# A decoder layer on one core: second up products by column halves, and the expert copies divided anew over three engines

## The chip, the cores and the metric

The kernel runs on one core of a Trainium2 chip. The metric is the device time of one execution in microseconds (us), the median of several runs; lower is better. The engines are TensorE (PE in the profile, its weight loads PEld), VectorE (DVE), ScalarE (ACT), GpSimd (POOL) and SyncE (SP, here only a DMA queue). An engine's name with a q behind it is that engine's own sequencer: register loads, waits, branches.

## The reference

16 sequences of 256 rows and 256 columns pass one decoder layer, all float32. What matters here is its third part, a mixture of 64 experts with two layers. Four rows of 256 make one token of 1024 values, so a sequence has 64 tokens.

```python
def kmoe(x_flat, W_router, A, B, scale, bias, d_in1, d_in2, d_out1, d_out2, top_k):
    logits = x_flat @ W_router.T
    vals, idx = jax.lax.top_k(logits, top_k)
    probs = jax.nn.softmax(vals, axis=-1)
    xs = x_flat.reshape(-1, d_in1, d_in2)
    Ag = A[idx]
    Bg = B[idx]
    Y = jnp.einsum('nkoi,nij,nkpj->nkop', Ag, xs, Bg)
    out = jnp.einsum('nkop,nk->nop', Y, probs).reshape(-1, d_out1 * d_out2)
    return out * scale + bias
...
x = x + _L0_attn_ref(_layernorm(x, axis=-1), ...)    # Fourier mixing, running sum over rows
x = x + _L0_xattn_ref(_layernorm(x, axis=-1), ctx_1024, ctx_1024, ...)    # 16 heads of 64
x = x + _L0_ffn_ref(_layernorm(x, axis=-1), ...)    # kmoe up 32x32 to 64x64, gelu, kmoe down
```

Each token picks two experts (k = 0, 1) in the up layer and two in the down layer. For each, a first product with B (32x64 up, 64x32 down) and a second with A are made, weighted by the softmax of the two logits.

## The kernel before, in words

Everything stays in SBUF but the rows in and out. The loop is staggered: one pass does the attention parts of sequence b and the expert parts of sequence c = b - 1. The list ORDER, written out by hand, sets the order of all steps; each engine walks through the list and does its own share of each step, in that order, so an engine that waits holds back all its later steps. A pass falls into four stretches, named here for the rest of the document:

- the start: `k_proj`, the layer norms, `logits_up`, `route_top_up`, `f_proj`, `route_up`, `product_kv`
- the up stage: steps `("up", g)` for g from 0 to 17, with `("choose", (g + 3, 0))` behind each, and single steps of the attention beside them (`v_proj`, `Q`, `inverse`, `power`, `fpower`, `x1`, `ln2_stats`, `ln2`, `ln2_turn`, `q_proj`)
- `logits_dn`, 32 matmuls of 64 columns over the hidden values `h`
- the heads: steps `("head", i)` for i from 0 to 19, with the down layer between them: `choose` (from i = 2, half of a group at each), `dn_first` at odd i from 5, `dn_second` at even i from 6; then the products with `wo` and `final`

The up layer has 16 groups of 4 tokens. A group's experts are gathered by copies inside SBUF: `choose_up` makes 8 copies (unit = 2 * token + k) of 32 partitions by 128 elements from `experts` into one of 5 buffers `chosen_up`, at a column that comes from a register. The registers are filled by `fetch_offsets`, one load for four groups, in the engine's own sequencer (L246). CHOOSERS divides the units: POOL takes unit 0, DVE 1 to 3, ACT 4 to 7. Then in `up(c, g)`:

- PE makes the first product of group g, two float32 records on 128x128 (L777), into one of three banks FA, FB, S0
- DVE weighs it by the route probabilities into W (`weigh`, L1019)
- PE, two steps later, makes the second product (L788): for each k one matmul of 128 rows by 64 columns with 256 moving columns, summed over k, into partitions 0 to 63 or 64 to 127 of bank G by the group's parity
- DVE scales it and adds the bias into `pre` (L1032, 64 partitions by 256)
- ACT makes the gelu twice into `h`, once plain (L560) and once shifted (L563)

A float32 matmul shows in the trace as two records, so L788 has four in a group. The down layer has 8 groups of 8 tokens; `choose_dn` copies 16 units of 64 partitions by 64 elements, DVE 0 to 7 and ACT 8 to 15, four of each in either half of the step. Its first products (L801) use the two row halves in turn, its second ones (L815) have 32 output columns. `head` on DVE masks the scores (L908), copies every second transposed block of probabilities for PE (L901) and normalises; on PE it transposes (L690), makes scores (L717, L719) and the products with the values (L701 to L704).

GpSimd makes the roots of the layer norms (`deviation`, L388 and L390), half of the Fourier products (`cross`, L404 to L413), `fpower_root`, two bias sums, and its one copy of each up group. `hold(engine, passed, sem, value)` is a wait on a semaphore followed by an increment of `passed`: the engine's sequencer goes no further until the value is there.

Of the kernel before, what the change touches and what calls it, by code (L numbers as in the profile page):

```python
# [23 lines left out]
ACT = mybir.ActivationFunctionType  # L24
# [48 lines left out]
def decoder_layer(nc, t, out):  # L73
    ctx = ExitStack()
    with ctx:
# [25 lines left out]
        experts_up, experts_dn = experts[0:D1, :], experts[F1:P, 0:EXPERTS * 2 * D1]  # L101
# [39 lines left out]
        pre_both = sb("pre", [P, UP_TOK * F1])  # L141
        pre = [pre_both[i * F1:(i + 1) * F1, :] for i in (0, 1)]
# [9 lines left out]
        yT = sb("yT", [P, CT, SEQ])  # L152
        W = [sb(f"W{i}", [P, A_DN // 2]) for i in (0, 1)]
# [7 lines left out]
        route_diag = sb("route_diag", [F1, 2 * TOKENS * TOPK])  # L161
# [57 lines left out]
        FFN_LOADS = 9  # L219
# [33 lines left out]
        def choose_up(copy, held, g, units):  # L253

            to = chosen_up[g % UP_SLOTS]
            for unit in units:
# [4 lines left out]
                src = experts_up[:, bass.ds(held[g % LOADED, unit], 2 * F1)]  # L261
# [66 lines left out]
        def _(sp):  # L328
# [33 lines left out]
            for dst, name in ((experts_up, "experts_up"), (experts_dn, "experts_dn"), (bias_up[:, :], "bias_up"),  # L362
# [13 lines left out]
        def _(pool):  # L376
            pool.memset(vals[:, :, :, KEY:KEY + 1], 1.0).then_inc(vals_ones, 1)
# [7 lines left out]
            def deviation(b, k):  # L385
# [4 lines left out]
                pool.tensor_tensor(rstd[:, k, :], var_eps[:, k, :], inv_root[:, :], ALU.pow).then_inc(ln_rstd[k], 1)  # L390

            def fpower_root(b):
# [4 lines left out]
                pool.tensor_scalar(fnorm[:, :], fnorm[:, :], 1e-9, None, ALU.add).then_inc(fnorm_step, 1)  # L397

            def cross(b, k, left, left_sem, left_n, right):
# [13 lines left out]
                pool.memset(prodA[0:1, 256:512], 0.0).then_inc(lane_fixed, 1)  # L413

            def bias_x1(b):
# [22 lines left out]
            def route_up(c):  # L438
                hold(pool, passed, offsets_ready, at(c, 2, 1))

            steps = {"choose": choose, "route_up": route_up,
# [4 lines left out]
                     "fpower": fpower_root, "ln2_turn": bias_x1, "logits_up": bias_x2}  # L446
# [3 lines left out]
        def _(act):  # L450
# [103 lines left out]
            def up(c, g):  # L554
                g -= UP_SKEW
                if g < 0:
                    return
                act.wait_ge(hidden_in, at(c, 16, g + 1))
                cols = slice(g * UP_TOK * F1, (g + 1) * UP_TOK * F1)
                act.activation(h[0:F1, cols], pre[g % 2], ACT.Gelu).then_inc(h_ready, 1)  # L560
# [558 lines left out]
```

## Time and profile before

| | |
|---|---|
| time, median of 3 runs | 2172.82 us (2169.03 to 2178.83) |
| the profiled execution's own time | 2180.39 us |
| its span, first to last instruction | 2178.5 us |
| mean granted TensorE clock | 0.927 of full speed |
| PE busy | 1947.4 us (89%) |
| DVE busy | 1283.8 us (59%) |
| ACT busy | 1252.4 us (57%) |
| POOL busy | 277.6 us (13%) |

Busy time is the union of an engine's instructions; the records of matmuls run into one another and their ends are modelled. A full pass lasts about 132 us and there are 15 of them with both halves, one half pass ahead and one behind.

### The profile page before, as it was taken

To read this page: it belongs to the slowest core of one execution; us is meant where nothing else is said; L and a number is where in the kernel's file an instruction comes from. 1 tells how busy PE (TensorE), PEld (TensorE's weight loads), DVE (VectorE), ACT (ScalarE), POOL (GpSimd) and SP (SyncE) were. 2 spreads that over 40 slices of the span, in tenths; PEclk is the share of its full clock that TensorE was granted. 3 is DMA by queue.
4 is the path that set the end of the run, shared out by engine and by line. 5 is a ranking of instruction groups with operands and counts; after the bars stand their busy time and mean duration, and the time that the engine had idled before them with its cause. 6 is when DMAs were issued, how large, how long until landed. Compare 5 with 4: busy or idle time off the path is not lost.

```text
span 2178.5 us, 47368 instructions
## 1 busy us (share of the span) xinstructions
PE 1947.4 (89%) x13298; PEld 1458.5 (67%) x13298; DVE 1283.8 (59%) x5457; ACT 1252.4 (57%) x4007; POOL 277.6 (13%) x593
## 2 busy tenths in 40 slices
PE   7998988989898989988989889888989999899975
PEld 5767667675766757667676676767767577675754
DVE  1456555666565666656565556665656656566664
ACT  2475564757556485564755547565474755648553
POOL 3020200203021030200202002020110302102010
PEclk9998999999999898989989899898998989989887
DMA  7000000000000000000000000000000000000000
GB/s 226 1 11 1 7 11 8 11 2 16 2 7 11 7 11 1 7 11 8 11 2 7 11 8 11 2 16 2 7 11 2 16 2 7 11 7 2 1 6 6
DMA packets 18600, 27.65 MB, mean 13 GB/s; under 512 B 2178, under 2 KB 17027, under 8 KB 17923
## 3 DMA queue, kind: packets, MB, share of 16 engines
q1 hardware_dynamic: 18274, 23.84, 3.4%
q8 instruction: 140, 2.29, 0.4%
q14 instruction: 186, 1.52, 0.2%
HBM read 19.65 MB, written 4.19 MB: 11 GB/s over the span
## 4 chain that ended last, share of the span: by engine, by line
PE 63%; DVE 14%; issue 12%; ACT 4%; DVEq 3%; POOL 2%; ACTq 1%; POOLq 0%
PE G L788 7%; PE O L732 5%; PE G L759 5%; PE PT L690 4%; PE G L815 4%; PE S L719 3%; PE S L717 3%; PE S L632 3%; DVE chosen_dn L275 2%; PE S L642 2%; DVE yT L1042 2%; DVE shared L908 2%; PE FA L801 2%; PE PT L672 2%; ACT chosen_up L262 1%
## 5 line engine op out<-in xcount | busy, mean ns | idle before, releaser
L508 ACT ACTIVATE shared<-shared,neg_max 128x128 f32<-128x128 f32 (+1 forms) x512 | 204.9, 447 | 297.8 <-DVE neg_max L908 296.4
L262 ACT COPY chosen_up<-experts 32x128 f32 x1024 | 251.6, 291 | 44.9 <-issue 38.5
L788 PE MATMUL G<-chosen_up,W 128*64 128x256 f32 x1024 | 260.5, 394 | 8.0 <-DVE pre L1032 8.0
L908 DVE CUSTOM_DVE_ANT_0 shared<-S,neg_bias 128x128 f32<-128x128 f32 (+1 forms) x512 | 162.4, 355 | 127.7 <-PE S L719 122.1
L690 PE MATMUL PT<-ident,shared 128*128 128x128 f32 x768 | 161.0, 326 | 77.9 <-DVE shared L901 65.1
L275 ACT COPY chosen_dn<-experts 64x64 f32 x1024 | 197.7, 240 | 52.9 <-issue 36.5
L275 DVE COPY chosen_dn<-experts 64x64 f32 x1024 | 152.4, 189 | 67.6 <-issue 57.5
L262 DVE COPY chosen_up<-experts 32x128 f32 x768 | 171.9, 255 | 32.3 <-issue 27.1
L388 POOL TENSOR_SCALAR var_eps<-moments 128x2 f32<-128x2 f32 x48 | 10.4, 217 | 1355.7 <-DVE moments L845 1345.5
L1032 DVE SCALAR_TENSOR_TENSOR pre<-G,scale_up,bias_up 64x256 f32<-64x256 f32 x256 | 123.2, 481 | 87.5 <-PE G L788 79.8
L815 PE MATMUL G<-chosen_dn,W 128*32 128x64 f32 x2048 | 157.5, 237 | 18.5 <-DVE W L1019 18.5
L1042 DVE COPY yT<-G 32x64 f32<-32x64 f32 x512 | 111.6, 218 | 100.5 <-PE G L815 86.9
L690 PEld LDWEIGHTS PT<-ident,shared 128*128 128x128 f32 x768 | 95.6, 162 | 110.7 <-issue 86.4
L788 PEld LDWEIGHTS G<-chosen_up,W 128*64 128x64 f32 x1024 | 113.0, 137 | 79.5 <-DVE W L1019 9.8
L815 PEld LDWEIGHTS G<-chosen_dn,W 128*32 128x32 f32 x2048 | 135.0, 121 | 33.9 <-issue 16.1
L467 ACT ACTIVATE kT<-S,bk 128x256 f32<-128x256 f32 x64 | 26.9, 470 | 193.8 <-PE S L609 193.8
L560 ACT ACTIVATE h<-pre 64x256 f32<-64x256 f32 x256 | 106.1, 415 | 34.9 <-DVE pre L1032 28.7
L759 PEld LDWEIGHTS G<-r_dn,h 128*64 128x64 f32 x1024 | 115.0, 204 | 6.8 <-issue 5.0
L732 PE MATMUL O<-wo,qT 128*128 128x256 f32 x512 | 118.7, 385 | 0.0
L759 PE MATMUL G<-r_dn,h 128*64 128x64 f32 x1024 | 117.2, 276 | 1.4 <-ACT h L563 1.4
L948 DVE MAX8 top_val<-G 64x8 f32<-64x64 f32 x32 | 7.2, 225 | 175.4 <-PE G L759 139.1
L262 POOL COPY chosen_up<-experts 32x128 f32 x256 | 78.3, 315 | 245.3 <-PE G L788 228.3
(164 smaller groups left out, 3819.4 us busy)
## 6 DMA issues: line engine op xcount, KB each, us to landing
x<-in_x SPq DMA_DIRECT2D x16, 256.0 KB, 2.7
ctxT<-in_ctxT SPq DMA_DIRECT2D x16, 256.0 KB, 2.9
out<-xn SPq DMA_DIRECT2D x16, 256.0 KB, 3.1
neg_bias<-in_neg_bias SPq DMA_DIRECT2D x1, 2048.0 KB, 13.3
wk<-in_xWk SPq DMA_DIRECT2D x1, 1024.0 KB
wo<-in_xWo SPq DMA_DIRECT2D x1, 1024.0 KB
wv<-in_xWv SPq DMA_DIRECT2D x1, 1024.0 KB, 7.7
wq<-in_xWq SPq DMA_DIRECT2D x1, 1024.0 KB, 9.7
```

What stands on the lines that cost most here:

```text
L262: last = copy(dst, src.rearrange("p (m c) -> p m c", m=2))
L275: last = copy(dst, src.rearrange("p (m c) -> p m c", m=2))
L508: act.activation(probs[i % 3][:, lo:hi], probs[i % 3][:, lo:hi], ACT.Exp, bias=neg_max[:, i % 3, rt:rt + 1], scale=-1.0).then_inc(probs_re ...
L560: act.activation(h[0:F1, cols], pre[g % 2], ACT.Gelu).then_inc(h_ready, 1)
L690: mm = pe.transpose(PT[:, j * P:(j + 1) * P], probs[e % 3][:, j * P:(j + 1) * P], ident[:, :])
L732: mm = pe.matmul(O[:, rt * 256:(rt + 1) * 256], qT[:, m, rt * P:(rt + 1) * P], wo[:, m, :], start=(m == 0), stop=(m == PAIRS - 1))
L759: mm = pe.matmul(G[0:F1, 0:EXPERTS], cols[:, 0, q, :], r_dn[:, q, :], start=(q == 0), stop=(q == F1 // 2 - 1))
L788: mm = pe.matmul(G[g % 2 * F1:(g % 2 + 1) * F1, 0:n], up_W(g)[:, k * F1:(k + 1) * F1], chosen_up[g % UP_SLOTS][:, k * n:(k + 1) * n], star ...
L815: mm = pe.matmul(G[g % 2 * F1:g % 2 * F1 + D1, u * 2 * D1:(u + 1) * 2 * D1], W[g % 2][:, n * D1:(n + 1) * D1], chosen_dn[g % DN_SLOTS][:, ...
L908: dve.tensor_tensor_reduce(probs[i % 3][:, lo:hi], S[i % 2][:, lo:hi], neg_bias[:, i, (1 - rt) * P:2 * P], 1.0, TOP, ALU.add, ALU.min, neg ...
L1032: dve.scalar_tensor_tensor(pre[g % 2].rearrange("p (n o) -> p n o", o=F1), G[side, 0:n].rearrange("p (n o) -> p n o", o=F1), scale_up[side ...
L1042: dve.tensor_copy(yT[il * D1:(il + 1) * D1, :, g * rows:(g + 1) * rows], y[:, il]).then_inc(y_kept, 1)
```

## The change

1. The second up products are made for two neighbouring groups at once, at every odd step: four matmuls, of which the first and third write partitions 0 to 63 of G and the other two partitions 64 to 127. The `pre` of both groups is then one DVE instruction on 128 partitions, and ACT makes four gelus in a row. `pre` now lies in `yT`. PE gets a wait for W of three groups ago ahead of a first product.
2. The copies are divided anew. Up: POOL units 0 to 3 (tokens 0 and 1), DVE 4 and 5, ACT 6 and 7. Down: by DN_TOKEN, POOL takes the four odd tokens (8 units, partitions 64 to 127), DVE tokens 0 and 2, ACT tokens 4 and 6 (4 units each). The up experts lie twice in `experts`, on partitions 0 to 31 and 32 to 63, and a token's parity picks the copy that is read. There are 6 buffers `chosen_up`.
3. POOL also takes part in the down `choose` (all 8 units in the first half of the step) and has a hold at the end of `deviation`, `fpower_root`, `cross`, the bias sums and each up `choose`, so that it waits for its own last instruction before the next step.
4. `xn3T` is stored by ACT with the four rows of a token apart, so that the weights of `logits_up` are read from neighbouring elements; `own_parts` reads it accordingly. `route_diag` and a block of ones lie in the unused columns of `experts`, and the down offsets are sorted by the new shares.

```diff
-UP_SLOTS, DN_SLOTS = 5, 3
+UP_SLOTS, DN_SLOTS = 6, 3
 UP_SKEW = 2
+UP_PAIRS = UP_GROUPS // 2
...
-CHOOSERS = {"pool": {"up": range(0, 1), "dn": range(0, 0)},
-            "dve": {"up": range(1, 4), "dn": range(0, 8)},
-            "act": {"up": range(4, 8), "dn": range(8, 16)}}
+CHOOSERS = {"pool": {"up": range(0, 4), "dn": range(8, 16)},
+            "dve": {"up": range(4, 6), "dn": range(0, 4)},
+            "act": {"up": range(6, 8), "dn": range(4, 8)}}
+DN_TOKEN = (0, 2, 4, 6, 1, 3, 5, 7)
...
-                src = experts_up[:, bass.ds(held[g % LOADED, unit], 2 * F1)]
+                src = experts_up[n % 2][:, bass.ds(held[g % LOADED, unit], 2 * F1)]
...
             def choose(c, n_part):
 
-                n = n_part[0]
+                n, part = n_part
+                if part == 0:
+                    fetch_offsets(held, mybir.EngineType.Pool, n, "pool")
                 if n < UP_GROUPS:
-                    fetch_offsets(held, mybir.EngineType.Pool, n, "pool")
                     if n >= UP_SLOTS:
                         hold(pool, passed, second_done, at(c, GROUPS, n - UP_SLOTS + 1))
                     choose_up(pool.tensor_copy, held, n, CHOOSERS["pool"]["up"]).then_inc(chosen_pool, 1)
+                    hold(pool, passed, chosen_pool, at(c, GROUPS, n + 1))
+                elif part == 0:
+                    g = n - UP_GROUPS
+                    if g >= DN_SLOTS:
+                        hold(pool, passed, second_done, at(c, GROUPS, n - DN_SLOTS + 1))
+                    choose_dn(pool.tensor_copy, held, g, CHOOSERS["pool"]["dn"]).then_inc(chosen_pool, 1)
+                    if g == DN_GROUPS - 1:
+                        hold(pool, passed, chosen_pool, at(c, GROUPS, n + 1))
...
-                act.copy(xn3T[:, :, :], FA[:, :].rearrange("p (c s) -> p c s", c=CT)).then_inc(xn3T_ready, 1)
+                act.copy(xn3T[:, :, :].rearrange("p c (r n) -> p c n r", r=UP_TOK),
+                         FA[:, :].rearrange("p (c n r) -> p c n r", c=CT, r=UP_TOK)).then_inc(xn3T_ready, 1)
...
-                g -= UP_SKEW
-                if g < 0:
+                pair, odd = divmod(g - UP_SKEW, 2)
+                if pair < 0 or not odd:
                     return
...
-                        rows = xn3T[:, ct, :].rearrange("p (n r) -> p r n", r=UP_TOK)[:, r, :]
-                        mm = pe.matmul(G[0:F1, 0:EXPERTS], rows, r_up[:, n, :], start=(n == 0), stop=(n == 2 * UP_TOK - 1))
+                        mm = pe.matmul(G[0:F1, 0:EXPERTS], xn3T[:, ct, r * TOKENS:(r + 1) * TOKENS], r_up[:, n, :], start=(n == 0), stop=(n == 2 * UP_TOK - 1))
...
-                    pe.wait_ge(chosen_pool, at(c, UP_GROUPS, g + 1))
+                    pe.wait_ge(chosen_pool, at(c, GROUPS, g + 1))
+                    if g >= 3:
+                        pe.wait_ge(W_ready, at(c, GROUPS, g - 2))
...
-                g -= UP_SKEW
-                if g >= 0:
-                    pe.wait_ge(W_ready, at(c, GROUPS, g + 1))
-                    if g >= 2:
-                        pe.wait_ge(hidden_in, at(c, 16, g - 1))
+                pair, odd = divmod(g - UP_SKEW, 2)
+                if pair >= 0 and odd:
+                    pe.wait_ge(W_ready, at(c, GROUPS, 2 * pair + 2))
+                    if pair >= 1:
+                        pe.wait_ge(hidden_in, at(c, UP_PAIRS, pair))
                     else:
                         pe.wait_ge(pm_ready, at(c, 6, 4))
                     n = UP_TOK * F1
                     for k in range(TOPK):
-                        mm = pe.matmul(G[g % 2 * F1:(g % 2 + 1) * F1, 0:n], up_W(g)[:, k * F1:(k + 1) * F1],
-                                       chosen_up[g % UP_SLOTS][:, k * n:(k + 1) * n], start=(k == 0), stop=(k == TOPK - 1))
-                    mm.then_inc(second_done, 1)
+                        for j in (0, 1):
+                            of = 2 * pair + j
+                            mm = pe.matmul(G[j * F1:(j + 1) * F1, 0:n], up_W(of)[:, k * F1:(k + 1) * F1],
+                                           chosen_up[of % UP_SLOTS][:, k * n:(k + 1) * n], start=(k == 0), stop=(k == TOPK - 1))
+                            if k == TOPK - 1:
+                                mm.then_inc(second_done, 1)
...
                 pe.wait_ge(chosen_act, at(c, GROUPS, UP_GROUPS + g + 1))
+                pe.wait_ge(chosen_pool, at(c, GROUPS, UP_GROUPS + g + 1))
...
-                    dve.scalar_tensor_tensor(pre[g % 2].rearrange("p (n o) -> p n o", o=F1),
-                                             G[side, 0:n].rearrange("p (n o) -> p n o", o=F1),
-                                             scale_up[side, 0:1], spread(bias_up[side, :], 1, UP_TOK),
+                    dve.scalar_tensor_tensor(pre[pair % 2].rearrange("p (n o) -> p n o", o=F1),
+                                             G[:, 0:n].rearrange("p (n o) -> p n o", o=F1),
+                                             scale_up[:, 0:1], spread(bias_up[:, :], 1, UP_TOK),
                                              ALU.mult, ALU.add).then_inc(hidden_in, 1)
```

## Rows read from the trace of the kernel before

**Rows 1.** Windows over three passes' heads: length, PE busy, clock, DMA share, GB/s.

```profile
428.52:490.48 61.96, 55.93 (x531) 0.94 0.01 2
1088.01:1154.08 66.07, 60.19 (x531) 0.87 0.01 2
954.31:1021.66 67.35, 61.65 (x531) 0.85 0.01 2
```

**Rows 2.** Windows of 2 us in the heads of one pass, same columns.

```profile
1096.00:1098.00 2.00, 0.00 (x1) 0.97 0.00 0
1098.00:1100.00 2.00, 1.53 (x9) 0.50 0.00 0
```

**Rows 3.** Timeline, same heads: start, us, instruction, count, idle time before and its releaser.

```profile
1097.13 0.64 DVE L275 COPY chosen_dn<-experts 64x64 f32 x4 [1.79 <-issue]
...
1098.47 0.90 PE L690 MATMUL PT<-ident,shared 128*128 128x128 f32 x3 [2.47 <-DVE shared L901]
...
1124.48 0.54 PE L690 MATMUL PT<-ident,shared 128*128 128x128 f32 x3 [1.88 <-DVE shared L901]
```

**Rows 4.** Line 246, the offset loads: ns min/median/max, first and last start, of each sequencer.

```profile
L246 ACTq TENSOR_LOAD <-offsets x96: 1009/1022/1969, 115.0 to 2150.7; - x96
L246 DVEq TENSOR_LOAD <-offsets x96: 845/858/2104, 115.1 to 2154.9; - x96
L246 POOLq TENSOR_LOAD <-offsets x64: 315/321/522, 117.0 to 2116.6; - x64
```

**Rows 5.** Chain that ended last, 428 to 492 us: shares by line.

```profile
by line: issue 16.6%; PE O L732 11.4%; DVE chosen_dn L275 7.5%; DVE yT L1042 5.9%; DVE shared L908 5.7%; PE PT L690 4.3%; PE S L719 4.2%; PE S L717 3.9%; PE G L815 3.2%; PE FA L672 3.0%; PE FB L672 3.0%; DVEq L246 2.7%; PE FA L801 2.6%; PE 
```

**Rows 6.** Window over one up stage: us, busy PE, PEld, DVE, ACT, POOL, clock, DMA.

```profile
1045.50:1080.70 35.20, 32.18 (x142) 18.66 (x140) 24.82 (x88) 31.32 (x99) 9.91 (x24) 1.00 0.05 16
```

**Rows 7.** Chain in the same up stage: start, us, what.

```profile
1055.46 0.42 PE S L777 x2
1055.88 1.01 PE G L788 x4
```

**Rows 8.** Timeline of PE in the heads: products on one or on two halves.

```profile
1088.26 0.60 PE L719 MATMUL S<-kT,qT 64*128 64x256 f32 x4
...
1111.22 0.68 PE L801 MATMUL FB<-chosen_dn,h 64*64 64x64 f32 x16
...
1114.23 1.08 PE L815 MATMUL G<-chosen_dn,W 128*32 128x64 f32 x16
```

**Rows 9.** Timeline of POOL, start and up stage.

```profile
1044.16 0.99 POOL L262 COPY chosen_up<-experts 32x128 f32 x2 [0.26 <-issue]
1045.86 1.24 POOL L404 TENSOR_TENSOR shared<-shared 128x256 f32<-128x256 f32 x1 [0.70 <-DVE shared L867]
...
1049.00 0.80 POOL L262 COPY chosen_up<-experts 32x128 f32 x3
...
1062.14 0.70 POOL L395 TENSOR_TENSOR fnorm<-fpower,root 128x2 f32<-128x2 f32 x1 [0.98 <-DVE fpower L882]
...
1063.89 0.28 POOL L262 COPY chosen_up<-experts 32x128 f32 x1 [0.30 <-issue]
...
1069.05 0.29 POOL L262 COPY chosen_up<-experts 32x128 f32 x1 [1.56 <-PE G L788]
```

**Rows 10.** Timeline of DVE beside POOL's products, then line 262's range on DVE.

```profile
1046.43 1.57 DVE L262 COPY chosen_up<-experts 32x128 f32 x3
...
L262 DVE COPY chosen_up<-experts x768: 203/216/749, 116.3 to 2124.3; 32x128 f32 x192
```

**Rows 11.** Groups of the whole trace, gelus: busy us, mean ns, idle before.

```profile
L560 ACT ACTIVATE h<-pre 64x256 f32<-64x256 f32 x256 | 106.1, 415 | 34.9 <-DVE pre L1032 28.7
...
L563 ACT ACTIVATE h<-pre 64x192 f32<-64x192 f32 x256 | 92.3, 360 | 6.2
```

**Rows 12.** Timeline of PE: the two logits.

```profile
1033.90 2.13 PE L752 MATMUL G<-r_up,xn3T 128*64 128x64 f32 x16
...
1080.68 5.52 PEld L759 LDWEIGHTS G<-r_dn,h 128*64 128x64 f32 x49 [0.33 <-issue]
```

More of the change, by code:

```diff
@@ L152, in decoder_layer @@
         yT = sb("yT", [P, CT, SEQ])
+        pre = [yT[:, i, :] for i in (0, 1)]
         W = [sb(f"W{i}", [P, A_DN // 2]) for i in (0, 1)]
@@ L218, in decoder_layer @@
         ATTN_LOADS = 4
-        FFN_LOADS = 9
+        FFN_LOADS = 10
         block = ctx.enter_context(nc.Block())
@@ L390, in deviation @@
                 pool.tensor_tensor(rstd[:, k, :], var_eps[:, k, :], inv_root[:, :], ALU.pow).then_inc(ln_rstd[k], 1)
+                hold(pool, passed, ln_rstd[k], at(b, 2, 2))
             def fpower_root(b):
@@ L397, in fpower_root @@
                 pool.tensor_scalar(fnorm[:, :], fnorm[:, :], 1e-9, None, ALU.add).then_inc(fnorm_step, 1)
+                hold(pool, passed, fnorm_step, at(b, 2, 2))
             def cross(b, k, left, left_sem, left_n, right):
@@ L413, in cross @@
                 pool.memset(prodA[0:1, 256:512], 0.0).then_inc(lane_fixed, 1)
+                hold(pool, passed, lane_fixed, at(b, 6, 3 * k + 3))
             def bias_x1(b):
@@ L419, in bias_x1 @@
                 pool.tensor_tensor(x1[:, :, :], x1[:, :, :], spread(out_bias[:, :], 1, RT), ALU.add).then_inc(x1_biased, 1)
+                hold(pool, passed, x1_biased, at(b, 1, 1))
             def bias_x2(c):
@@ L436, in choose, with route @@
                     choose_up(pool.tensor_copy, held, n, CHOOSERS["pool"]["up"]).then_inc(chosen_pool, 1)
-            def route_up(c):
-                hold(pool, passed, offsets_ready, at(c, 2, 1))
-            steps = {"choose": choose, "route_up": route_up,
+                    hold(pool, passed, chosen_pool, at(c, GROUPS, n + 1))
[6 more added lines that the diff above has]
+                        hold(pool, passed, chosen_pool, at(c, GROUPS, n + 1))
+            def route(c, layer):
+                hold(pool, passed, offsets_ready, at(c, 2, layer + 1))
+            steps = {"choose": choose, "route_up": lambda c: route(c, 0),
                      "ln1": lambda b: deviation(b, 0), "ln3": lambda c: deviation(c, 2),
@@ L554, in up @@
             def up(c, g):
[L555 to L556 removed]
+                pair, odd = divmod(g - UP_SKEW, 2)
+                if pair < 0 or not odd:
                     return
[L558 to L563 removed]
+                act.wait_ge(hidden_in, at(c, UP_PAIRS, pair + 1))
+                for j in (0, 1):
+                    cols = slice((2 * pair + j) * UP_TOK * F1, (2 * pair + j + 1) * UP_TOK * F1)
+                    hidden = pre[pair % 2][j * F1:(j + 1) * F1, :]
+                    act.activation(h[0:F1, cols], hidden, ACT.Gelu).then_inc(h_ready, 1)
+                    above = h[F1:P, cols].rearrange("p (u c) -> p u c", c=2 * F1)[:, :, 0:2 * F1 - F1 // 2]
+                    shifted = hidden.rearrange("p (u c) -> p u c", c=2 * F1)[:, :, F1 // 2:2 * F1]
+                    act.activation(above, shifted, ACT.Gelu).then_inc(h_ready, 1)
             steps = {"k_proj": k_proj, "ln1_turn": lambda b: keep_xnT(b, 1), "f_proj": f_proj, "v_proj": v_proj,
@@ L972, in route_keep @@
                 of = G[0:1, 256:384].rearrange("p (g u) -> p g u", g=groups)
+                by_half = G[0:1, 256:384].rearrange("p (g t half k) -> p half g t k", g=groups, half=2, k=TOPK)
                 for name in CHOOSERS:
@@ L976, in route_keep @@
                         to = offsets[:, start:start + groups * len(units)].rearrange("p (g u) -> p g u", g=groups)
-                        last = dve.tensor_copy(to, of[:, :, units.start:units.stop])
+                        if layer == 0:
+                            last = dve.tensor_copy(to, of[:, :, units.start:units.stop])
+                        else:
+                            half, first = divmod(units.start // TOPK, DN_TOK // 2)
+                            some = by_half[:, half, :, first:first + len(units) // TOPK, :]
+                            last = dve.tensor_copy(to.rearrange("p g (t k) -> p g t k", k=TOPK), some)
                 last.then_inc(offsets_ready, 1)
```

40 lines of the change are left out of this document (20 added, 20 removed).

## The prediction

> **What bounds the kernel now.** I read the page first. It puts TensorE far ahead of the others, but a full pass is made of stretches with different limits, and two of them are touched.
>
> The heads come first. Windows over the heads of three passes [rows 1] show the same work in 61.96, 66.07 and 67.35 us; what differs is the granted clock: 0.94, 0.87, 0.85. Between the levels 2.4 and 1.2 GHz a mean clock of 0.94 is 12% of the stretch at the low one, 7.4 us; 0.85 is 30%, 20.2 us. So 12.8 us more at the low level cost 5.4 us, 0.42 us each, and the middle row agrees (17.2 us low, 66.1 forecast). With no low clock the heads would take 61.96 - 3.1 = 58.9 us. The windows of 2 us [rows 2] show what went before: TensorE did nothing for 2 us, then the clock stood at 0.50. The timeline [rows 3] names the cause: DVE's down copies start after 1.79 us of issue, L901 behind them is late, and TensorE waits 2.47 us for it; eight heads later the same again, 1.88 us. The 1.79 us are the offset load of 32 values in DVE's sequencer [rows 4]. Where no load falls, the chain of waits through the heads [rows 5] runs over DVE as much as over PE: its down copies are 7.5% of it.
>
> The up stage is different: PE is busy 32.18 of 35.20 us at clock 1.00, ACT 31.32, DVE 24.82 and POOL only 9.91 [rows 6]. A group costs PE 0.42 us for the first product and 1.01 us for the second [rows 7], so 16 groups are 22.9 of the 32.2 us; the rest is the attention's. In its second half ACT, with two gelus (0.415 and 0.360 us [rows 11]) and four copies a group, is as long as PE.
>
> **The change, part by part.** Everything is counted against the profiled execution: 2180.4 us, of which 2178.5 are span; the median of the runs is 7.6 us lower.
>
> Column halves. In the heads, where neighbouring products use different halves of the array, 16 records of L801 take 0.68 us, while 16 of L815, all on one part of the columns, take 1.08 [rows 8]; in L719 four records with 256 columns on two row halves take 0.60 us, against 1.01 for four of L788. No row shows halves of columns alone. If they overlap like the row halves, a pair costs 0.95 to 1.1 us instead of 2.02; if not, 2.02 as now. I take 1.0. Per pass PE loses 8 x 1.0 = 8 us of work in the up stage, and DVE makes 8 `pre` on 128 partitions for 16 on 64. This is a gain only as far as no other engine sets the pace.
>
> Who sets it then. Per group ACT has two copies fewer, about 0.8 + 0.5 = 1.3 us; DVE one fewer and half a `pre`. POOL has four copies for one. From its rows [rows 9]: three copies in a row take 0.80 us, 0.26 apart, so four take 1.05; after a hold and a wait the next copy starts some 0.30 us later. A group is 1.35 us. The load of 16 values, by 60 ns a value (ACT 16 to 32 values, 1.009 to 1.969 us [rows 4]) on top of POOL's 0.32 for 4, is 1.04 us, and with the new hold nothing covers it. None of this is queued behind PE: the sixth buffer leaves POOL free to run ahead. So POOL's own queue sets the stage, and I follow it in the times of the pass shown. Its copies began at 1044.16. The load adds 0.7 and the hold 0.15; the earlier Fourier products (below) take back 0.5: 1044.5. Group 0 beside DVE's running sums, where two copies took 0.99 [rows 9], takes 1.5, group 1 1.35: 1047.4. Then `product_q` is ahead of group 2 in the queue, 1045.86 to 1049.00 before, 3.14 us: 1050.7 with its hold. 14 groups at 1.35 are 18.9, three loads 3.1, `fpower_root` 1.2 (1062.14 to the copy before the one at 1063.89): 1073.9.
>
> What contention adds is bounded from below by nothing. From above: beside POOL's Fourier products DVE's three copies took 1.57 us, 0.52 each [rows 10], against a median of 0.216, so the two engines do hold each other up. DVE now has two copies of 0.22 a group; if POOL meets each of them half way, 0.15 to 0.2 a group, 2.1 in all. The last copy ends at 1076.0 instead of 1069.34 [rows 9]. The Trainium skill (SBUF — State Buffer, "Who interferes with whom") states that a VectorE copy of this kind and a GpSimd operation lock one port pair for the whole instruction, the loser fully blocked; the 0.52 us agree, and by a full block of every DVE copy by POOL the sum would only gain 0.2 us a group more.
>
> Behind the last copy. Before, 11.3 us passed from it to `logits_dn` (1069.34 to 1080.68 [rows 9, 12]). PE then still had five second products, 5.05 us; now it has two pairs, 2.0. But `ln2` stands on POOL behind the last `choose`, and DVE waits there for the root, with all its later weighing: root and small operation 1.17, as in `fpower_root`, and DVE's norm 0.8, 2.0 us in which PE has no work. 11.3 - 3.05 + 2.0 = 10.3. So `logits_dn` starts at 1086.3, 5.6 later than now; with some low clock after PE's many short waits I take 6.0 per pass, 96 us for 16. Four gelus in a row, 1.55 us, lie beside the last `q_proj`.
>
> Start. L752's 16 records take 2.13 us [rows 12], against 1.08 for L815's [rows 8] with weights side by side in memory: 1.0 us less on PE. ACT's copies into `own` stand between this and the Fourier products, so I count half, already used above. ACT's spread write of `xn3T` and the other read pattern in `own_parts` I take at nothing: same element counts; were they a tenth longer, 0.4 us of ACT there, under what is left over.
>
> Heads. DVE's load falls from 32 to 16 values: 1.259 us for 20 values [rows 4], 63 ns each, so 1.0 us less; and two of four copies at 0.16 go [rows 3], 0.3. Both idle times of PE shrink by 1.3 us, to 1.2 and 0.6. The up stage has 3.0 us idle at clock 1.00 throughout [rows 6], so I expect the clock to hold: 66.1 - 7.2 - 2.6 = 56.3 us. POOL now has 8 copies a group (under 0.28 each, 2.1 us and two loads of 2.0) in some 5.3 us of heads, covered by its idle time; `dn_first` of a group comes three heads after its `choose`. It will meet DVE's copies, 0.8 us. Sum -9.0 a pass, bounds -2.6 (the clock still falls) and -11 (DVE's 16 other copies a pass, 2.6 us on its part of the chain, are won as well); 15 passes, -135 us.
>
> Sum: 2180.4 + 96 - 135 = 2141.4, less 7.6: 2134 us.
>
> **The rivals.**
> - GpSimd's copies are cheaper than their pitch of 0.26 us. For: units 0 and 1 use partitions 0 to 31, units 2 and 3 partitions 32 to 63, and all its rows are on 0 to 31. If the pairs overlap, four take 0.7 us, 14 x 0.35 = 4.9 us a pass less, up stage +1.1: 2180.4 + 18 - 135 - 7.6 = 2055. The Trainium skill (GPSIMD Engine Reference, "Instruction dispatch") states that each of its cores serves 16 partitions and goes to the next instruction when its own share is done, which would give this result; no run here shows it yet.
> - The other side: GpSimd is slower still. For: the pair at 1044.16 took 0.50 us a copy [rows 9]. If copies average 0.33, the stage loses another 14 x 0.28 = 4 us, +10, and PE, waiting at every group, falls to the low clock before the heads, which then win only 6: 2180.4 + 160 - 90 - 7.6 = 2243. It decides from +8.4 us in the up stage on, where a group costs 0.17 us more than I count.
> - The heads keep the low clock, because 1.2 us idle still suffices or POOL's copies lengthen it. Then they win 2.6 us: 2134 + 15 x 6.4 = 2230; one of the two falls avoided, 2182. Against: PE's idle time halves in one and falls to a third in the other.
> - The change doesn't do what it says, the column halves run one after the other: two pairs behind the last copy cost 2.1 us more, 2134 + 34 = 2168; the rest hides behind POOL.
>
> **How the numbers follow.** Forecast 0.40, cheap GpSimd 0.18, slow GpSimd 0.17, low clock kept 0.18, no overlap 0.07. A change within 0.5% (2162 to 2184) is about what this kernel's measurement can't tell from none. The forecast's own range, 2095 to 2175, is mostly faster (0.36) with 0.03 in the band and 0.01 slower; cheap GpSimd is 0.18 faster; no overlap 0.02, 0.04 and 0.01; low clock 0.02, 0.05 and 0.11; slow GpSimd 0.17 slower. Together 0.58, 0.12, 0.30. The range 2045 to 2235 takes in the forecast, both halves of the low clock and parts of the two GpSimd cases.
>
> **What would show it.** Right: L788 in pairs of some 1.0 us for eight records; PE in the up stage waiting for POOL's `chosen_up`, POOL busy nearly throughout it; the stage 5 to 7 us longer; the offset loads near 1.1 us on DVE and 1.0 and 2.0 on POOL; idle times of 1.2 and 0.6 us ahead of L690 and heads near 57 us at clock 1.00; L752's weight loads near 0.11 us. Wrong: POOL's copies far from 0.26 us apart in the up stage, or a clock under 0.9 in the heads.

## The result, and the profile after

The changed kernel takes 2233.3 us (median of 4 runs, 2223.26 to 2236.03), the kernel before 2175.75 us beside it (4 runs): a ratio of 1.0245, 95% interval 1.0214 to 1.0276. It is slower; 2134 us was forecast. The profiled execution took 2233.06 us, its span is 2231.3 us.

The page first, with parts 1, 2 (PE and its clock) and 4:

```profile
PE 1882.9 (84%) x13298; PEld 1419.6 (64%) x13298; DVE 1130.3 (51%) x4577; ACT 1029.6 (46%) x2983; POOL 662.5 (30%) x2387
PE   7979788897898979889798897988979788797965
PEclk9988979889798988989889798897989889888977
...
PE 47%; issue 18%; POOL 13%; DVE 9%; POOLq 5%; ACT 4%; DVEq 1%
POOL chosen_up L264 8%; PE G L780 5%; PE O L754 5%; PE G L842 5%; PE PT L712 4%; PE S L741 3%; PE S L739 3%; POOLq L248 3%; PE G L813 2%; PE O L631 2%; DVE yT L1074 2%; PE PT L694 2%; DVE shared L935 2%; PE FA L828 2%; POOL rstd L395 2%
```

VectorE and ScalarE lost 150 and 220 us of work, GpSimd gained 385, and GpSimd's up copies now lead the chain. To see where the time went, the windows over one pass, cut at the first `logits_up`, the first up product, `logits_dn`, the first head, `final` and the next `logits_up` (us, busy PE, PEld, DVE, ACT, POOL, clock, DMA share, GB/s):

```profile
1059.72:1072.44 12.72, 10.85 (x52) 7.25 (x51) 6.91 (x28) 9.04 (x25) 4.53 (x10) 1.00 0.00 1
1072.44:1112.39 39.95, 30.26 (x141) 18.30 (x141) 16.81 (x62) 23.08 (x67) 21.36 (x70) 0.83 0.04 14
1112.39:1119.72 7.33, 7.33 (x66) 7.26 (x66) 0.00 (x0) 2.09 (x3) 0.00 (x0) 1.00 0.01 2
1119.72:1182.72 63.00, 58.65 (x531) 47.74 (x532) 39.00 (x175) 25.81 (x85) 11.84 (x64) 0.89 0.01 2
1182.72:1197.04 14.32, 10.37 (x46) 8.20 (x44) 8.02 (x22) 4.15 (x8) 3.19 (x5) 0.88 0.07 22
```

Cut the same way, from the starts of these lines in each trace, the means over the 15 full passes are below ("end" is from `final` to the next `logits_up`, a mean of 14). The rows below the first two are experiments of the next section. One of e7's five executions (2092.83 us), the one with the trace, ran disturbed at a lower clock; it doesn't count in e7's ratio, and e7 has no row here. "Low" is the part of the up stage and of the heads, in us, that TensorE spent at 1.2 GHz.

| kernel | start | up stage | low | heads | low | end | time, us |
|---|---|---|---|---|---|---|---|
| before | 11.60 | 35.25 | 0.2 | 66.14 | 17.3 | 12.43 | 2175.75 |
| after | 12.82 | 40.03 | 14.6 | 62.11 | 12.3 | 14.07 | 2233.3 |
| e1 down copies held | 12.77 | 40.49 | 16.9 | 54.77 | 0.0 | 13.12 | 2118.57 |
| e9 down copies drained | 12.78 | 40.46 | 16.0 | 55.71 | 1.8 | 13.46 | 2133.14 |
| e8 = e1, no norm hold | 12.81 | 40.33 | 16.2 | 54.77 | 0.0 | 12.54 | 2108.5 |
| e5 = e1, single products | 12.77 | 38.86 | 1.8 | 55.04 | 0.9 | 12.84 | 2089.4 |
| e6 = e5, old up shares | 11.60 | 35.21 | 0.5 | 55.03 | 0.9 | 14.20 | 2042.14 |
| e10 = e6, no norm hold | 11.60 | 35.64 | 1.8 | 55.03 | 0.9 | 13.56 | 2038.02 |
| e11 = e10, old layout | 11.60 | 35.59 | 0.5 | 56.34 | 3.9 | 13.87 | 2061.03 |
| e12 = e10, pairs | 11.61 | 36.41 | 15.5 | 54.73 | 0.0 | 12.63 | 2029.43 |
| e2 = after, single products | 12.84 | 39.04 | 2.7 | 62.06 | 12.1 | 14.17 | 2228.31 |
| e3 = after, old division | 11.60 | 36.56 | 17.5 | 65.69 | 17.8 | 13.33 | 2210.26 |
| e4 = after, old layout | 13.43 | 41.21 | 20.0 | 61.38 | 10.7 | 14.38 | 2253.75 |

After against before, a full pass: start +1.2, up stage +4.8, heads -4.0, end +1.6; 15 x 2.0 + 14 x 1.6 = 53 us, the difference of the two spans (52.8).

**The heads.** The timeline of the same pass, POOL, DVE and PE, answers to [rows 3]:

```profile
1125.87 4.36 POOL L278 COPY chosen_dn<-experts 64x64 f32 x24 [21.32 <-issue]
...
1127.84 2.44 DVE L278 COPY chosen_dn<-experts 64x64 f32 x2 [0.78 <-issue]
1130.20 0.54 DVE L928 COPY shared<-PT 128x384 f32<-128x384 f32 x1
...
1130.88 0.54 PE L712 MATMUL PT<-ident,shared 128*128 128x128 f32 x3 [3.10 <-DVE shared L928]
1131.48 0.80 PE L739 MATMUL S<-kT,qT 64*128 64x128 f32 x4
...
1157.08 0.54 PE L712 MATMUL PT<-ident,shared 128*128 128x128 f32 x3 [0.55 <-DVE shared L928]
```

VectorE's issue time fell from 1.79 to 0.78 us, as forecast. But GpSimd finds its first three buffers free and makes all their 24 copies in one run; VectorE's two copies come 2 us into it and take 2.44 us. L928 (L901 before) is late, TensorE waits 3.10 us for it, more than the 2.47 of before, and behind it L739 takes 0.80 us, where a head earlier it took 0.49: the clock is at 1.2 GHz. Eight heads later the wait is 0.55 us, and the clock stays at 1.00 from there to the end of the heads. The instructions of the line that copies, ns min/median/max:

```profile
L278 POOL COPY chosen_dn<-experts x1024: 229/248/306, 173.7 to 2219.1; 64x64 f32 x171
...
L278 DVE COPY chosen_dn<-experts x512: 177/189/2434, 175.7 to 2221.8; 64x64 f32 x171
```

Fifteen of VectorE's 512 copies last 2107 to 2434 ns, one in each full pass; a sixteenth, in the last half pass, 709.

**The up stage.** Timeline of POOL (it answers to [rows 9]) and PE, in order of time:

```profile
1078.09 0.46 PE L800 MATMUL S<-chosen_up,own 128*128 128x128 f32 x2 [1.53 <-POOL chosen_up L264]
...
1080.60 1.08 POOL L264 COPY chosen_up<-experts 32x128 f32 x4 [1.33 <-issue]
1081.92 1.12 POOL L264 COPY chosen_up<-experts 32x128 f32 x4 [0.24 <-POOL chosen_up L264]
1083.38 1.08 POOL L264 COPY chosen_up<-experts 32x128 f32 x4 [0.34 <-POOL chosen_up L264]
...
1087.49 1.08 PE L813 MATMUL G<-chosen_up,W 128*64 128x256 f32 x8
...
1094.62 0.46 PE L800 MATMUL S<-chosen_up,own 128*128 128x128 f32 x2 [2.29 <-DVE W L1052]
...
1099.25 1.98 PE L813 MATMUL G<-chosen_up,W 128*64 128x256 f32 x8
1100.06 1.08 POOL L264 COPY chosen_up<-experts 32x128 f32 x4 [0.34 <-POOL chosen_up L264]
```

A GpSimd group is 1.08 + 0.34 = 1.42 us, and a load puts about 1.3 us ahead of it. In this pass TensorE waits four times for GpSimd's copies, 4.6 us in all, and once, 2.29 us, for W. L813's eight records take 1.08 us, where four of L788 took 1.01 [rows 7]: the column halves overlap almost fully. At the low clock they take 1.98.

**The end.** Timeline of POOL, ACT and PE:

```profile
1189.37 0.71 POOL L395 TENSOR_TENSOR rstd<-var_eps,inv_root 128x2 f32<-128x2 f32 x1
1190.46 0.22 POOL L393 TENSOR_SCALAR var_eps<-moments 128x2 f32<-128x2 f32 x1 [0.37 <-POOL rstd L395]
1191.68 1.05 ACT L536 COPY xn3T<-FA 128x512 f32<-128x512 f32 x1 [1.15 <-PE FA L763]
1193.34 1.11 PE L644 MATMUL TR<-ident,xn 128*128 128x128 f32 x4 [1.70 <-DVE xn L878]
1194.25 2.86 PE L631 MATMUL O<-ctxT,wk 128*128 128x256 f32 x8
1197.04 1.15 PE L773 MATMUL G<-r_up,xn3T 128*64 128x64 f32 x16
```

The same places of the kernel before (the ACT row is of the pass ahead of this one):

```profile
1030.33 0.59 ACT L517 COPY xn3T<-FA 128x512 f32<-128x512 f32 x1 [0.73 <-PE FA L741]
...
1163.82 0.66 PE L622 MATMUL TR<-ident,xn 128*128 128x128 f32 x4 [1.29 <-DVE xn L851]
1164.31 1.89 PE L609 MATMUL O<-ctxT,wk 128*128 128x256 f32 x8
```

The second norm now waits for GpSimd to finish the first, TensorE waits 1.70 us where it waited 1.29, and then it too runs slower: four records take 1.11 us and took 0.66, the next eight take 2.86 and took 1.89. The spread write of `xn3T` takes 1.05 us, the plain one took 0.59. What the new layout gives is the last row of the upper block, 1.15 us for 2.13 [rows 12]. In the mean of the 14 stretches TensorE is at the low level for 3.1 us, for 0.5 before; in the two that hold 1.00 the end takes 12.8 us, 0.6 more than those of before that hold it (12.2).

### The profile page after: what moved, and what is told of

The parts are those of the page before. It is cut to its first block, busy times and chain, and to the rows that moved or that the text cites. A ratio compares the mean times of both kernels' runs of the same rounds, so it can differ in the third digit from the quotient of the medians.

```text
span 2231.3 us, 47686 instructions
## 1 busy us (share of the span) xinstructions
PE 1882.9 (84%) x13298; PEld 1419.6 (64%) x13298; DVE 1130.3 (51%) x4577; ACT 1029.6 (46%) x2983; POOL 662.5 (30%) x2387
## 3 DMA queue, kind: packets, MB, share of 16 engines
q8 instruction: 140, 2.29, 0.4%
## 4 chain that ended last, share of the span: by engine, by line
PE 47%; issue 18%; POOL 13%; DVE 9%; POOLq 5%; ACT 4%; DVEq 1%
POOL chosen_up L264 8%; PE G L780 5%; PE O L754 5%; PE G L842 5%; PE PT L712 4%; PE S L741 3%; PE S L739 3%; POOLq L248 3%; PE G L813 2%; PE O L631 2%; DVE yT L1074 2%; PE PT L694 2%; DVE shared L935 2%; PE FA L828 2%; POOL rstd L395 2%
## 5 line engine op out<-in xcount | busy, mean ns | idle before, releaser
L278 POOL COPY chosen_dn<-experts 64x64 f32 x1024 | 189.5, 253 | 777.1 <-PE G L842 437.0
L264 POOL COPY chosen_up<-experts 32x128 f32 x1024 | 280.7, 298 | 172.5 <-issue 92.8
L712 PE MATMUL PT<-ident,shared 128*128 128x128 f32 x768 | 153.2, 313 | 62.3 <-DVE shared L928 54.7
L582 ACT ACTIVATE h<-yT 64x256 f32<-64x256 f32 x256 | 106.4, 415 | 214.8 <-DVE yT L1064 210.1
L813 PE MATMUL G<-chosen_up,W 128*64 128x256 f32 x1024 | 181.6, 488 | 0.7 <-DVE yT L1064 0.7
L712 PEld LDWEIGHTS PT<-ident,shared 128*128 128x128 f32 x768 | 91.0, 155 | 91.8 <-issue 62.9
L842 PEld LDWEIGHTS G<-chosen_dn,W 128*32 128x32 f32 x2048 | 126.0, 115 | 25.9 <-DVE W L1052 10.2
L264 ACT COPY chosen_up<-experts 32x128 f32 x512 | 118.5, 292 | 35.7 <-DVE offsets L1006 31.1
L393 POOL TENSOR_SCALAR var_eps<-moments 128x2 f32<-128x2 f32 x48 | 10.4, 217 | 392.1 <-DVE moments L872 372.3
L278 DVE COPY chosen_dn<-experts 64x64 f32 x512 | 109.7, 255 | 31.8 <-issue 25.3
L1064 DVE SCALAR_TENSOR_TENSOR yT<-G,scale_up,bias_up 128x256 f32<-128x256 f32 x128 | 61.7, 482 | 124.1 <-PE G L813 122.6
L264 DVE COPY chosen_up<-experts 32x128 f32 x512 | 105.1, 249 | 23.1 <-issue 15.7
L278 ACT COPY chosen_dn<-experts 64x64 f32 x512 | 98.2, 240 | 34.1 <-PE G L842 20.3
L800 PE MATMUL FA<-chosen_up,own 128*128 128x128 f32 x192 | 55.1, 378 | 65.9 <-POOL chosen_up L264 37.7
```

What stands on the lines that cost most here:

```text
L264: last = copy(dst, src.rearrange("p (m c) -> p m c", m=2))
L278: last = copy(dst, src.rearrange("p (m c) -> p m c", m=2))
L582: act.activation(h[0:F1, cols], hidden, ACT.Gelu).then_inc(h_ready, 1)
L712: mm = pe.transpose(PT[:, j * P:(j + 1) * P], probs[e % 3][:, j * P:(j + 1) * P], ident[:, :])
L813: mm = pe.matmul(G[j * F1:(j + 1) * F1, 0:n], up_W(of)[:, k * F1:(k + 1) * F1], chosen_up[of % UP_SLOTS][:, k * n:(k + 1) * n], start=(k = ...
L842: mm = pe.matmul(G[g % 2 * F1:g % 2 * F1 + D1, u * 2 * D1:(u + 1) * 2 * D1], W[g % 2][:, n * D1:(n + 1) * D1], chosen_dn[g % DN_SLOTS][:, ...
```

## The experiments

**1. The down copies held back (e1).** GpSimd begins a down group only when VectorE has made its copies of it, so its first 24 copies no longer come in one run.

```diff
                     if g >= DN_SLOTS:
                         hold(pool, passed, second_done, at(c, GROUPS, n - DN_SLOTS + 1))
+                    hold(pool, passed, chosen_dve, at(c, GROUPS, n + 1))
```

> Edit: GpSimd starts its down copies of a group only when VectorE has made its own of that group. Theory (GpSimd's 24 copies in a row keep VectorE's down copies waiting 2.44 us, TensorE then idles 3.10 us and its clock falls): the pair of VectorE copies takes 0.3 us, TensorE's wait ahead of L712 shrinks to 1.0 to 1.3 us, the clock holds in the heads, heads about 57.5 instead of 62.3 us a pass: 2233 - 15 x 4.8 = 2161 us. Rival (an idle time of 1.2 us lets the clock fall as well): only the 1.9 us of idle time go, 2205 us. Rival (VectorE is late for its own offset load): no change, 2233 us.

Measured 2118.57 us, ratio 0.9718 (0.9666 to 0.977). The line's row on VectorE, and the clock in the heads, with e5's window (the same hold) for a look at the columns:

```profile
L278 DVE COPY chosen_dn<-experts x512: 179/190/261, 178.1 to 2108.1; 64x64 f32 x171
```

```profile
1060.00:1114.60 54.60, 52.49 (x530) 42.81 (x531) 36.82 (x175) 25.69 (x85) 11.95 (x64) 1.00 0.01 2
```

No copy is over 261 ns, the clock stays at 1.00, TensorE's wait ahead of the products of L712 is 0.98 us, and the heads take 54.8 us in every pass. One wait, added, is worth 115 us, where 72 were expected: the heads are 2.7 us shorter than the 57.5 put for them. It also delays GpSimd's copies, so it doesn't yet say whether their meeting VectorE's is the trouble or the length of the run.

**2. Drained after each down group (e9).** GpSimd starts as early as in the changed kernel, but waits for its own last copy after every group.

```diff
-                    if g == DN_GROUPS - 1:
-                        hold(pool, passed, chosen_pool, at(c, GROUPS, n + 1))
+                    hold(pool, passed, chosen_pool, at(c, GROUPS, n + 1))
```

> Edit: the changed kernel with a hold behind each of GpSimd's down groups of 8 copies, not only behind the last, so that its first three groups run as 1.5 us, a pause of 0.3, 1.5 us and so on instead of 4.36 us without a pause. Theory (VectorE's copy can't begin while GpSimd's copies follow one another without a gap, and gets in at the first gap): VectorE's longest down copy falls from 2.4 us to at most 1.5, TensorE's wait of 3.1 us by 0.8 or more; as the clock may still fall, 2190 to 2225 us. Rival (it waits for one GpSimd copy at a time, and something else made it late): no copy changes, 2233 us.

Measured 2133.14 us, 0.9763 (0.9737 to 0.9789), far under what was expected; only in three passes does the clock still fall in the heads, for 7 to 14 us. Timeline of POOL, DVE and PE, the copies' timeline first:

```profile
1093.09 1.48 POOL L278 COPY chosen_dn<-experts 64x64 f32 x8 [21.26 <-issue]
1094.82 1.50 POOL L278 COPY chosen_dn<-experts 64x64 f32 x8 [0.24 <-POOL chosen_dn L278]
1095.06 0.40 DVE L278 COPY chosen_dn<-experts 64x64 f32 x2 [0.78 <-issue]
1096.06 0.54 PE L711 MATMUL PT<-ident,shared 128*128 128x128 f32 x3 [1.06 <-DVE shared L927]
```

And the line's own row on VectorE:

```profile
L278 DVE COPY chosen_dn<-experts x512: 177/189/259, 179.3 to 2125.2; 64x64 f32 x171
```

The copies still meet: VectorE's two start 0.24 us into a GpSimd run and take 0.40 us together. So meeting is harmless; what costs is the long run. In this trace 72 of VectorE's copies start inside a run of 8, all but one at most 0.93 us after its beginning (the one at 1.47, as the run ends), and take 0.19 to 0.26 us. In the changed kernel those in runs of 8 do the same (the longest 0.30 us), and those that start 1.97 us into the run of 24 are held until its last copy. Where between 0.97 and 1.97 us the blocking sets in was not tried. The 24 copies follow each other every 0.177 us, but single ones grow from 0.235 us at the start of a run to 0.26 at its eighth and 0.30 at its twenty-fourth: they overlap more and more. That no gap is left for VectorE is likely, and only argued. The Trainium skill (SBUF — State Buffer, "Who interferes with whom") lets the engine that comes second wait for the whole instruction of the other; by that rule the wait would end after one copy, 0.3 us. The changed kernel's 2.28 us are a wait for all that is left of a run, and the 0.22 and 0.26 us of the two copies shown here are hardly a wait at all.

**3. Single second products (e2 from the changed kernel, e5 from e1).** Second products, `pre` and gelus are made group by group again, as before; the division of the copies stays.

```diff
-                pair, odd = divmod(g - UP_SKEW, 2)
-                if pair >= 0 and odd:
+                g -= UP_SKEW
+                if g >= 0:
...
-                        for j in (0, 1):
-                            of = 2 * pair + j
-                            mm = pe.matmul(G[j * F1:(j + 1) * F1, 0:n], up_W(of)[:, k * F1:(k + 1) * F1],
+                        mm = pe.matmul(G[g % 2 * F1:(g % 2 + 1) * F1, 0:n], up_W(g)[:, k * F1:(k + 1) * F1],
```

> Edit: the new division of the copies with the second up products made group by group as before. Theory (GpSimd sets the pace of the up stage, so the pairs win next to nothing there): the up stage grows by 2 to 3 us for the products behind the last copy, 2265 to 2285 us. Rival (the pairs' saved TensorE work counts in full, 8 us a pass): 2233 + 128 = 2360 us.

> Edit: GpSimd's down copies behind VectorE's, as in the first experiment, and the second up products group by group as before; the division of the changed kernel. Theory (the pairs win nothing: the TensorE time that they save in the up stage comes back as low clock): up stage 39.0 us against 40.5 with pairs, heads 54.8 in both, 2118 - 16 x 1.2 = 2100 us. Rival (the pairs are worth their 8 us of TensorE work where the clock is held): 2118 + 100 = 2220 us.

Measured e2 2228.31 us, 1.0236 (1.0178 to 1.0295), against the changed kernel's 1.0245: no difference clear of noise; e5 2089.4 us, 0.957 (0.9531 to 0.9609), 29 us under e1. Under GpSimd's pace the pairs cost time: the stage is 38.9 us without them and 40.5 with, low for 1.8 and 16.9 us. The loss expected of e2 didn't come. Window of e5's up stage, and its last copies and `logits_dn`:

```profile
1013.60:1052.60 39.00, 33.59 (x140) 19.58 (x140) 20.97 (x70) 23.40 (x66) 21.35 (x70) 0.96 0.04 14
```

```profile
1041.21 1.08 POOL L264 COPY chosen_up<-experts 32x128 f32 x4 [0.34 <-PE G L810]
...
1052.66 1.54 PE L779 MATMUL G<-r_dn,h 128*64 128x64 f32 x12
```

From the end of GpSimd's last copy to `logits_dn` it is 1052.66 - 1042.29 = 10.4 us without pairs and, in the changed kernel, 1112.39 - 1101.14 = 11.25 with them. In the mean of the 15 full passes it is 10.2 in e2 and e5, 11.3 in the changed kernel, 11.5 in e1 and 11.4 in the kernel before.

**4. The old up shares (e6), and two, three, three (e7).** From e5, GpSimd makes one up copy a group again, VectorE three, ScalarE four, and the hold after GpSimd's up copies goes; e7 gives GpSimd 2 and the others 3 each.

```diff
-CHOOSERS = {"pool": {"up": range(0, 4), "dn": range(8, 16)},
-            "dve": {"up": range(4, 6), "dn": range(0, 4)},
-            "act": {"up": range(6, 8), "dn": range(4, 8)}}
+CHOOSERS = {"pool": {"up": range(0, 1), "dn": range(8, 16)},
+            "dve": {"up": range(1, 4), "dn": range(0, 4)},
+            "act": {"up": range(4, 8), "dn": range(4, 8)}}
```

> Edit: e5 with the up copies divided as before the change (GpSimd 1, VectorE 3, ScalarE 4) and no hold behind each up choose; only the down copies are divided anew. Theory (GpSimd's four up copies set the pace of the up stage): up stage 35.2 us as before, clock 1.00, heads 54.8: 2100 - 16 x 4 - 10 = 2030 us. Rival (the longer start and the late layer norms, not the up copies, are what was lost): 2090 us.

> Edit: e6 with GpSimd 2, VectorE 3 and ScalarE 3 up copies. Theory (ScalarE was as long as TensorE in the second half of the old up stage; GpSimd at two copies a group, 0.85 us, has room): up stage 33.5 to 34.5 us, 10 to 25 us under e6. Rival (TensorE's 32.2 us of work and its short waits already fill the stage): the same as e6 within 5 us. Rival (more GpSimd copies lengthen VectorE's): 10 us over e6.

Measured e6 2042.14 us, 0.9379 (0.9313 to 0.9445): 47 us under e5, start -1.2 and up stage -3.7, end +1.4 a pass. The longer end goes with the clock: 3.4 us at the low level for 0.2. e7 2042.89 to 2056.65 us, 0.9384 (0.9335 to 0.9432): no difference from e6. Two, three, three gains nothing over one, three, four; four, two, two costs 47 us, together with the hold behind its copies, which no run takes out alone.

**5. The pairs with the old division (e3).** The changed kernel, with the copies, up and down, divided as before; the new layout stays.

```diff
+CHOOSERS = {"pool": {"up": range(0, 1), "dn": range(0, 0)},
+            "dve": {"up": range(1, 4), "dn": range(0, 8)},
+            "act": {"up": range(4, 8), "dn": range(8, 16)}}
```

> Edit: the pairs with the old division of the copies (GpSimd one up copy, ScalarE four; down copies on VectorE and ScalarE), all else as changed. Theory (eight records of a pair take 1.08 us instead of 2.02, then ScalarE with 31 us of work limits the up stage): up stage 35.2 to about 33 us, heads as before with their two falls of the clock, 66.2 us: 2180 - 2 x 16 + 10 for the slower start = 2150 to 2165 us. Rival (TensorE's work is the limit throughout): up stage 27 us, 2060 us. Rival (longer pairs add waits): 2180 or more.

Measured 2210.26 us, 1.0134 (1.008 to 1.0187), 45 us over the range expected; the rival with 2180 or more is the one that fits. Windows of its up stage and heads:

```profile
525.60:562.40 36.80, 33.04 (x141) 19.74 (x139) 20.61 (x79) 31.64 (x98) 10.05 (x24) 0.72 0.05 15
569.70:635.20 65.50, 60.37 (x531) 48.70 (x531) 39.87 (x206) 31.38 (x117) 0.00 (x0) 0.87 0.01 2
```

ScalarE is busy for 31.6 us, as before (31.32 [rows 6]), so little was to be gained beside it. The work that the pairs save on TensorE becomes short waits, the clock falls to a mean of 0.72 for 1.00, and what is left keeps TensorE busy for 33.04 us, for 32.18. The heads are those of before: the down division alone changes them.

**6. The old layout of `xn3T` (e4 from the changed kernel, e11 from e10).**

```diff
-                act.copy(xn3T[:, :, :].rearrange("p c (r n) -> p c n r", r=UP_TOK),
-                         FA[:, :].rearrange("p (c n r) -> p c n r", c=CT, r=UP_TOK)).then_inc(xn3T_ready, 1)
+                act.copy(xn3T[:, :, :], FA[:, :].rearrange("p (c s) -> p c s", c=CT)).then_inc(xn3T_ready, 1)
...
+                        rows = xn3T[:, ct, :].rearrange("p (n r) -> p r n", r=UP_TOK)[:, r, :]
```

> Edit: only the layout of xn3T as before; all else as changed. Theory: ScalarE's write of xn3T takes 0.59 instead of 1.05 us, the 16 records of logits_up 2.13 instead of 1.15 us; the first lies ahead of TensorE's second turn, the second ahead of the Fourier products, each partly covered: within 8 us of 2233. If the spread write is what makes the start longer: 2233 - 16 x 1 = 2217 us. If the faster logits carry the stage: 2233 + 16 = 2249 us.

> Edit: e10 with the old layout of xn3T as well. Theory (the same edit made the changed kernel 20 us slower: logits_up is a microsecond longer on TensorE while ScalarE's 0.46 us are partly covered): 2032 + 8 to 16 = 2044 us. Rival (with the up stage no longer waiting for GpSimd's start, ScalarE's spread write is what counts): 2025 us.

Measured e4 2253.75 us, 1.0315 (1.0252 to 1.0379); e11 2061.03 us, 0.945 (0.942 to 0.9479), against e10's 2038.02. The new layout is worth 23 us there, clear of noise and more than the 8 to 16 expected. From e4 to the changed kernel it is 20 us by the times and 15 by the ratios, whose intervals just overlap. ScalarE's slower write doesn't show: with the plain one the end is no shorter (14.4 us in e4 for 14.1, 13.9 in e11 for 13.6). In e4 the start is 0.6 and the up stage 1.2 us a pass longer; in e11 neither is, and its heads fall to the low clock in four passes for 13.7 us where e10's do in one. Why, no row shows.

**7. Without the hold at the end of `deviation` (e8 from e1, e10 from e6).**

```diff
-                hold(pool, passed, ln_rstd[k], at(b, 2, 2))
```

> Edit: the first experiment without the hold at the end of deviation. Theory (the hold puts the second root of the layer norms 0.4 us later, at three places of a pass, two of them at the start on the way to TensorE's turns): start 0.4 to 0.8 us a pass shorter, 2118 - 10 = 2108 us. Rival (the start is longer for ScalarE's spread write of xn3T alone): 2118 us.

> Edit: e6 (single second products, old up shares, down copies of GpSimd behind VectorE's) without the hold at the end of deviation. Theory (that hold costs about 0.6 us a pass, as it did in e8): 2042 - 10 = 2032 us. Rival (in e6 the stretch ahead of logits_up is longer for its low clock, and the hold hides): 2042 us.

Measured e8 2108.5 us, 0.966 (0.9622 to 0.9698); e10 2038.02 us, 0.936 (0.9339 to 0.938). The end is 0.6 us a pass shorter in both; that is 10 us in e8, whose four executions all lie below those of e1, and 4 in e10, less than its interval.

**8. The pairs in the best version (e12).** e10 with the second products in pairs, as in the changed kernel.

> The best version so far (2038 us: GpSimd's down copies held behind VectorE's, up shares 1, 3, 4, second up products group by group, no hold at the end of deviation) with one part of the change put back: the second up products in pairs. It tells what the pairs alone do where nothing else differs and the heads are undisturbed. Theory: the pairs overlap fully and take 8 us of TensorE's work out of the up stage, but the engine then has short waits between the pairs, falls to the low clock for 10 to 20 us of the stage, and the stage lasts 36.8 us for 35.1, as in the run with pairs and the old division; heads stay at 54.6. So 15 x 1.7 = 26 us more: 2055 to 2070. Rival: in the earlier run the low clock came from the disturbed pass, not from the pairs; then ScalarE's 31 us set the stage, it takes 32 to 34 us at clock 1.00, and the time is 2000 to 2025.

Measured 2029.43 us, 0.9317 (0.9294 to 0.934). The loss expected didn't come: it is 9 us under e10, and the intervals just touch. Windows of the up stage and the stretch behind the heads of a pass of e12, then of e10:

```profile
610.40:646.00 35.60, 31.31 (x142) 18.67 (x140) 20.69 (x79) 31.59 (x98) 9.51 (x24) 0.76 0.05 16
...
708.10:720.10 12.00, 8.88 (x45) 7.00 (x43) 7.95 (x22) 4.14 (x8) 3.19 (x5) 1.00 0.09 26
```

```profile
491.80:526.90 35.10, 32.05 (x141) 18.71 (x139) 24.34 (x87) 30.83 (x97) 9.96 (x24) 1.00 0.05 16
...
588.80:602.90 14.10, 10.77 (x46) 8.11 (x44) 8.01 (x22) 4.14 (x8) 3.19 (x5) 0.88 0.07 22
```

The up stage is longer, by 0.8 us in the mean, with 15.5 us at the low level, as the theory had it. It overlooked the rest of the pass: the end takes 12.6 us for 13.6, and in the pass shown it holds clock 1.00, where e10's has 0.88 (at the low level for 0.8 us in the mean, for 2.4). So e12 has more low clock than e10, but most of it lies where TensorE waits for ScalarE's copies anyway:

```profile
624.83 0.80 PE L799 MATMUL S<-chosen_up,own 128*128 128x128 f32 x2 [0.90 <-ACT chosen_up L264]
```

Why the end is spared is open. e12 is the fastest version measured, by little: the changed kernel's layout, pairs and down division, the old up shares, one hold added and two taken out.

## Why the prediction was wrong

The wrong step is in "Heads": "It will meet DVE's copies, 0.8 us", and with it "so I expect the clock to hold". The term was -9.0 us a pass and came out at -4.0: 15 x 5.0 = 75 of the 92 us between the sum (2141.4) and the profiled 2233.1. I priced GpSimd's copies by their number and their pitch and let them meet VectorE's one by one; I didn't ask when they would be issued. Three free buffers make it 24 in a row, and one copy of 0.19 us was held for 2.3. The idle time put at 1.2 us was 3.10; the second, put at 0.6, was 0.55. Experiments 1 and 2 show the cause: both break up or shift the run, keep every copy, and bring the heads to 54.8 and 55.7 us, below the 57.1 of the forecast. The rival "heads keep the low clock" had the right place and named GpSimd's copies as a way to it; its 2230 us was near, partly by luck, since it left the next term out.

The second miss is the end, +1.6 us a pass, 23 us, which isn't in the sum at all. The hold at the end of `deviation` is 0.6 us of it by experiment 7: item 3 of the change puts it on the path of both norms. The rest goes with the clock: 2.6 us more at the low level, 1.1 us by the prediction's own 0.42 each, an estimate. Taking ACT's spread write of `xn3T` "at nothing" was right for the time: it is 0.46 us longer, not the tenth allowed for, but the end is no shorter without it (experiment 6).

What was right: GpSimd's queue sets the up stage. Start and up stage together were put at +6.0 and are +1.2 + 4.8. A group was put at 1.35 and takes 1.42; the slow-GpSimd rival needed 0.17 more, not 0.07. The offset loads, put at 1.1 us on DVE and 1.0 and 2.0 on POOL (ns min/median/max):

```profile
L248 DVEq TENSOR_LOAD <-offsets x96: 593/602/1101, 114.8 to 2209.1; - x96
L248 POOLq TENSOR_LOAD <-offsets x96: 1048/1060/2033, 117.2 to 2206.5; - x96
```

The rival by which four GpSimd copies overlap to 0.7 us falls: they take 1.08, both halves of the partitions or not. The down copies, all on partitions 64 to 127, have a pitch of 0.177 us. The rival by which the column halves run one after the other falls too.

Near in size for a wrong reason: "Behind the last copy" lets the pairs save 3.05 us and adds 2.0 for `ln2`, 10.3 us for 11.3. In the mean it is 11.3 us, for 11.4 before, and 10.2 in e2 and e5 without pairs (experiment 3): here the pairs save nothing, and cost 1.0 to 1.3 us. That single second products fit into the waits of TensorE, and that the pairs leave it at the low clock, is the likely reason, not a shown one. The sum came out near because up to the last copy the pass is 6.1 us longer, for the 6.7 of the forecast, and because 0.4 us had been added for a low clock. In the whole study the pairs were worth between -29 us (e5 to e1) and +9 (e10 to e12, where the intervals touch). The gain of the change was the down division, which takes 11.4 us out of the heads once the run is broken up, and the layout.

## What to carry to other kernels

Ask of work that is moved to an idle engine not only how long it takes but when it will be issued: free buffers turn it into one burst, and a burst on GpSimd can hold a short VectorE copy until its end; a wait that costs nothing there was worth 5% here. TensorE time saved in a stretch that another engine sets was no gain in that stretch here, and came back as a lower clock; what it does to the stretches behind must be measured. When a change adds waits "for order", price each on the path it stands in.

## What the runs showed of the hardware

- A VectorE copy of 64x64 float32, 0.19 us alone, took 0.19 to 0.31 us when it started less than 1 us into a run of 8 GpSimd copies, and 2.1 to 2.4 us when it started 1.97 us into a run of 24: until about that run's last copy.
- Float32 products in the two column halves overlapped almost fully: eight records of 256 columns in 1.08 us, four in 1.01.
- GpSimd's copies from a column given by a register: four of 32x128 in 1.08 us, eight of 64x64 in 1.50, and 0.24 to 0.34 us more until the first copy after a hold on its own last one.
- ScalarE's copy of 128x512 from PSUM took 1.05 us with a write spread over four blocks, 0.59 with a plain one.
